# Nine attention stages on one core: the order of a step's work on TensorE, ScalarE and VectorE

## What is computed

```python
def _L2_xattn_ref(x1, x2, wq, wk, wv, wo, bo):
    q = (x1 @ wq.T).reshape(b, n, HEADS, HEAD_DIM).transpose(0, 2, 1, 3)
    k = (x2 @ wk.T).reshape(b, m, HEADS, HEAD_DIM).transpose(0, 2, 1, 3)
    v = (x2 @ wv.T).reshape(b, m, HEADS, HEAD_DIM).transpose(0, 2, 1, 3)
    dots = jnp.einsum('bhnd,bhmd->bhnm', q, k) * SCALE
    attn = jax.nn.softmax(dots, axis=-1)
    out = jnp.einsum('bhnm,bhmd->bhnd', attn, v)
    out = out.transpose(0, 2, 1, 3).reshape(b, n, DIM)
    return out @ wo.T + bo
...
x = x + _L2_xattn_ref(_layernorm(x, axis=-1), ctx_1024, ...)
```

## Time and profile before

| | us |
|---|---|
| median of 3 runs | 4896.71 |
| lowest, highest | 4893.21, 4901.27 |
| the profiled execution, its time | 4900.09 |
| the profiled execution, its span | 4898.2 |
| busy PE, DVE, POOL, ACT | 4007.7, 3203.4, 2994.6, 2059.5 |

### The profile page before, as it was taken

One profiled execution on the slowest core, in us unless ns is written; L12 is line 12 of the kernel. 1 busy time (PEld: TensorE's weight loads), 2 busy tenths in 40 slices (PEclk: granted clock), 3 DMA queues, 4 the chain that ended last, 5 costly groups with the idle time before them and its releaser, 6 DMA issues. The chain is left out here.

```text
span 4898.2 us, 215645 instructions
## 1 busy us (share of the span) xinstructions
PE 4007.7 (82%) x85067; PEld 2918.6 (60%) x85076; DVE 3203.4 (65%) x10848; ACT 2059.5 (42%) x5737; POOL 2994.6 (61%) x4949
## 2 busy tenths in 40 slices
PE   8999977254899978656999997559879998889988
PEld 6777754132566666523777774335547776667766
DVE  5875668422344688787556874753337878888866
ACT  4555545011344444365555554112225543336632
POOL 6766632276455699688556762038876777777710
PEclk9999988555899998755999997879998999999999
DMA  3000012433100022200000002113431000000000
GB/s 94 5 13 19 19 28 57 78 62 54 37 0 0 18 39 39 35 1 1 2 0 15 22 18 54 42 46 75 77 62 35 0 15 16 16 9 1 0 13 24
DMA packets 380509, 139.58 MB, mean 28 GB/s; under 512 B 216487, under 2 KB 373239, under 8 KB 380055
## 3 DMA queue, kind: packets, MB, share of 16 engines
q1 hardware_dynamic: 345430, 107.60, 9.3%
q0 software_dynamic: 34816, 28.34, 4.0%
HBM read 91.46 MB, written 43.85 MB: 28 GB/s over the span
## 5 line engine op out<-in xcount | busy, mean ns | idle before, releaser
L1051 DVE TENSOR_REDUCE rowmax<-ps 128x16 f32<-128x1024 f32 x512 | 626.3, 1223 | 488.0 <-PE ps L678 487.7
L696 PE MATMUL ps<-prob,kT 32*64 32x256 f32 x9216 | 781.7, 408 | 8.7 <-issue 2.4
L721 PE MATMUL ps<-v,probT 64*64 64x64 f32 x36864 | 764.6, 227 | 5.3 <-issue 2.2
L721 PEld LDWEIGHTS ps<-v,probT 64*64 64x64 f32 x36864 | 683.8, 140 | 57.4 <-issue 16.0
L678 PE MATMUL ps<-kblock,qT 32*64 32x256 f32 x8192 | 697.0, 410 | 17.2 <-DVE rowmax L1060 14.2
L900 ACT ACTIVATE probT<-ps 128x1024 f32<-128x1024 f32 x512 | 518.0, 1012 | 353.4 <-PE ps L708 353.0
L585 POOL TENSOR_TENSOR kblock<-kT,key_scale 128x512 f32<-128x512 f32 x576 | 599.8, 1041 | 18.2 <-ACT kT L878 7.6
L587 POOL TENSOR_TENSOR prob<-qT,key_scale 128x512 f32<-128x512 f32 x576 | 601.5, 1044 | 0.0
L561 POOL TENSOR_TENSOR vareps<-moments,eps 128x1 f32<-128x1 f32 x522 | 98.8, 189 | 745.7 <-DVE negmean L1025 745.6
L887 ACT ACTIVATE xn<-x_res,nmr,rstd 128x128 f32 (+1 forms) x512 | 252.7, 494 | 513.6 <-POOL nmr L567 349.5
L708 PEld LDWEIGHTS ps<-mT,pick_bf 32*64 32x64 bf16 x16384 | 311.7, 108 | 221.2 <-ACT mT L857 74.1
(11 more groups left out here) (380 smaller groups left out, 9655.7 us busy)
## 6 DMA issues: line engine op xcount, KB each, us to landing
ctxT<-in_ctxT SPq DMA_DIRECT2D x256, 64.0 KB, 1.8
held<-in_g_w SPq DMA_DIRECT2D x16, 836.0 KB
ctxT<-in_ctxT SPq DMA_DIRECT2D x256, 32.0 KB, 1.9
table<-prob SPq DMA_DIRECT2D x32, 256.0 KB, 2.4
x_dram<-x_res SPq DMA_DIRECT2D x32, 256.0 KB, 2.4
x_res<-x_dram SPq DMA_DIRECT2D x16, 512.0 KB, 6.9
x_res<-in_x SPq DMA_DIRECT2D x8, 512.0 KB, 7.5
x_res<-in_e_w SPq DMA_DIRECT2D x64, 64.0 KB
```

The source lines that it names most:

```text
L696: mm = nc.tensor.matmul(out.rearrange("p (h s) -> p h s", h=GH), k.kT[rows, buf, S * b:S * b + S], k.qblock[rows, buf, :, S * b:S * b + S] ...
L721: mm = nc.tensor.matmul(k.ps_o[S * b:S * b + S, u, S * hh:S * hh + S], k.probT[rows, buf, at:at + S], k.v9[rows, buf, (HD + 1) * h:(HD + 1 ...
L1051: nc.vector.tensor_reduce(spread, heads, AX.X, ALU.max).then_inc(soft.did["max_raw"], 1)
```

## The change

On TensorE a step now begins with queries and keys, the transposed `xn` and the transposed maxima; then come eight waits in a row; then y, the values and the transposed result; then mask rows and scores; the mixing is last. The first scores' bank is awaited by `max_raw` and no longer by `max_done`. The maxima are subtracted ahead of the second scores' products and no longer behind them. All softmax stages but L1_xattn make the values by one product, and the copies that take them out exchange the rows of heads 8 to 15: three instructions (128 x 64, and twice 64 x 64 elements) for one, on ScalarE or on VectorE. ScalarE does the front copies ahead of the value-side copies and no longer writes the doubled columns of `xnT`. VectorE does L1051's maxima ahead of the division, and the two differences last. In L3_xattn, the masked scores' addition stands in the place of the maxima.

```diff
--- before.py
+++ after.py
@@ -643,6 +643,15 @@
+WHOLE = (slice(0, P), slice(0, HEADS), slice(0, P))
...
+def value_parts():
+
+    first, second, low, high = slice(0, HEADS // 2), slice(HEADS // 2, HEADS), slice(0, S), slice(S, P)
+    return [(slice(0, P), first, slice(0, P)), (low, second, high), (high, second, low)]
...
-                    start=not part.softmax or first, stop=not part.softmax, tile_position=place)
+                    start=not part.softmax, stop=not part.softmax or groups == low, tile_position=place)
...
-                    start=False, stop=groups == low and h == GH - 1, tile_position=place)
+                    start=groups == high and h == 0 and not part.added, stop=False, tile_position=place)
...
-    def values_mixable(mixes, it, mb):
-        if mixes is not None:
-            after(pe, c, "exp_done", it, mb)
-            after(pe, c, "v_done", it, mb)
-            after(pe, c, "on_done", it, mb + 1)
-
-    def scores_writable(score1, score2, it):
-        if score1 is not None:
-            after(pe, c, "max_done", it, 4)
-            after(pe, c, "kblock_done", it, 3)
-        if score2 is not None:
-            after(pe, c, scores_read(c, it, 6), it, 6)
-            after(pe, c, "qblock_done", it, 5)
-
...
         less = score2 if score2 is not None and score2.softmax else None
 
         mm = None
-        if value is not None or turn is not None or out is not None:
-            after(pe, c, values_read(c, it, 4), it, 4)
-            after(pe, c, "y_read", it, 9)
-            after(pe, c, "oT_done", it, 8)
-        if out is not None:
-            mm = nc.tensor.matmul(k.ps_y, k.oT[:, b8, :], weights(out, 3), start=True, stop=True)
-        if value is not None:
-            source, wv = k.ctxT[:, b3, :] if value.cross else k.xnT[:, b3, :], weights(value, 2)
-            if value.softmax:
-                nc.tensor.matmul(k.ps_v[:, 0:S], source[:, 0:P], wv[:, 0:S], start=True, stop=True)
-                mm = nc.tensor.matmul(k.ps_v[:, S:P], source[:, S:S + P], wv[:, S:P], start=True, stop=True)
-            else:
-                mm = nc.tensor.matmul(k.ps_v, source[:, 0:P], wv, start=True, stop=True)
-        if turn is not None:
-            after(pe, c, "on_done", it, 7)
-            mm = nc.tensor.transpose(k.ps_oT, k.o[:, b7, :], k.ident)
-        if mm is not None:
-            mm.then_inc(c.yv_psum, 1)
-
-        mm = None
+        if mixes is not None:
+            after(pe, c, "v_done", it, mb)
         after(pe, c, "kT_done", it, 3)
         if c.steady is None:
...
-        early = less is None or any(part is not None and part.added for part in (score1, score2))
-        if less is None:
-            values_mixable(mixes, it, mb)
-            scores_writable(score1, score2, it)
         if norm is not None:
             after(pe, c, "xn_done", it, 1)
             mm = nc.tensor.transpose(k.ps_xT, k.xn[:, b1, :], k.ident)
         if less is not None:
-            values_mixable(mixes, it, mb)
-            if early:
-                scores_writable(score1, score2, it)
             after(pe, c, "max_done", it, 5)
             mm = nc.tensor.matmul(k.ps_mT, top_halves(k.rowmax[:, b5, :]), k.ident_bf[:, :], start=True, stop=True)
         if mm is not None:
             mm.then_inc(c.front_psum, 1)
 
+        mm = None
+        if score1 is not None:
+            after(pe, c, "max_raw", it, 4)
+            after(pe, c, "kblock_done", it, 3)
+        if score2 is not None:
+            after(pe, c, scores_read(c, it, 6), it, 6)
+            after(pe, c, "qblock_done", it, 5)
         if mixes is not None:
-            for hh in range(HEADS // 2):
-                mm = mix(mixes, (par - mb) % NB, hh)
-            mm.then_inc(mixes.did["o_psum"], 1)
-        if not early:
-            scores_writable(score1, score2, it)
+            after(pe, c, "exp_done", it, mb)
+        if value is not None or turn is not None or out is not None:
+            after(pe, c, values_read(c, it, 4), it, 4)
+            after(pe, c, "y_read", it, 9)
+            after(pe, c, "oT_done", it, 8)
+        if out is not None:
+            mm = nc.tensor.matmul(k.ps_y, k.oT[:, b8, :], weights(out, 3), start=True, stop=True)
+        if mixes is not None and turn is None:
+            after(pe, c, "on_done", it, mb + 1)
+        if value is not None:
+            source, wv = k.ctxT[:, b3, :] if value.cross else k.xnT[:, b3, :], weights(value, 2)
+            if value.name == "L1_xattn":
+                nc.tensor.matmul(k.ps_v[:, 0:S], source[:, 0:P], wv[:, 0:S], start=True, stop=True)
+                mm = nc.tensor.matmul(k.ps_v[:, S:P], source[:, S:S + P], wv[:, S:P], start=True, stop=True)
+            else:
+                mm = nc.tensor.matmul(k.ps_v, source[:, 0:P], wv, start=True, stop=True)
+        if turn is not None:
+            after(pe, c, "on_done", it, 7)
+            mm = nc.tensor.transpose(k.ps_oT, k.o[:, b7, :], k.ident)
+        if mm is not None:
+            mm.then_inc(c.yv_psum, 1)
+
         for bk in range(2):
             if score1 is not None and score1.added:
                 add_rows(score1, k.s1, 0, bk)
@@ -810,11 +804,11 @@
         if score1 is not None:
             query_scores(score1, b3, low).then_inc(score1.did["low_rows"], 1)
         if score2 is not None:
-            mm = key_scores(score2, b5, high, first=not score2.added)
             if less is not None:
                 after(pe, c, "mT_done", it, 5)
                 for h in range(GH):
-                    mm = less_max(less, b5, h, high)
+                    less_max(less, b5, h, high)
+            mm = key_scores(score2, b5, high)
             mm.then_inc(score2.did["first_rows"], 1)
 
         if score1 is not None:
@@ -822,11 +816,16 @@
             query_scores(score1, b3, high).then_inc(score1.did["s1_psum"], 1)
         if score2 is not None:
             after(pe, c, "first_rows", it, 5)
-            mm = key_scores(score2, b5, low, first=False)
             if less is not None:
                 for h in range(GH):
-                    mm = less_max(less, b5, h, low)
+                    less_max(less, b5, h, low)
+            mm = key_scores(score2, b5, low)
             mm.then_inc(score2.did["s2_psum"], 1)
+
+        if mixes is not None:
+            for hh in range(HEADS // 2):
+                mm = mix(mixes, (par - mb) % NB, hh)
+            mm.then_inc(mixes.did["o_psum"], 1)
...
-        if turn is not None:
-            act.wait_ge(c.yv_psum, it - 2)
-            after(act, c, "y_read", it, 8)
-            if c.name(it, 3) in VALUE_BIAS:
-                after(act, c, values_read(c, it, 3), it, 3)
-            nc.scalar.activation(k.oT[:, b7, :], k.ps_oT, ACT.Copy).then_inc(turn.did["oT_done"], 1)
-        if value is not None and value.name not in VALUE_BIAS:
-            act.wait_ge(c.yv_psum, it - 2)
-            after(act, c, "y_read", it, 8)
-            after(act, c, "o_psum", it, 3 + NB)
-            nc.scalar.activation(values(k, b3), heads_of(k.ps_v), ACT.Copy).then_inc(value.did["v_done"], 1)
...
-                if not norm.cross:
-                    nc.scalar.activation(k.xnT[:, b1, P:P + S], k.ps_xT[:, 0:S], ACT.Copy)
...
+        if turn is not None:
+            act.wait_ge(c.yv_psum, it - 2)
+            after(act, c, "y_read", it, 8)
+            if c.name(it, 3) in VALUE_BIAS:
+                after(act, c, values_read(c, it, 3), it, 3)
+            nc.scalar.activation(k.oT[:, b7, :], k.ps_oT, ACT.Copy).then_inc(turn.did["oT_done"], 1)
+        if value is not None and value.name not in VALUE_BIAS:
+            act.wait_ge(c.yv_psum, it - 2)
+            after(act, c, "y_read", it, 8)
+            after(act, c, "o_psum", it, 3 + NB)
+            for rows, heads, source in value_parts():
+                mm = nc.scalar.activation(values(k, b3)[rows, heads, :], heads_of(k.ps_v)[source, heads, :], ACT.Copy)
+            mm.then_inc(value.did["v_done"], 1)
...
-                nc.vector.tensor_tensor(values(k, b3), heads_of(k.ps_v), heads_of(bias),
-                                        ALU.add).then_inc(value.did["v_done"], 1)
+                for rows, heads, source in value_parts() if value.softmax else [WHOLE]:
+                    mm = nc.vector.tensor_tensor(values(k, b3)[rows, heads, :], heads_of(k.ps_v)[source, heads, :],
+                                                 heads_of(bias)[source, heads, :], ALU.add)
+                mm.then_inc(value.did["v_done"], 1)
...
+        if soft is not None:
+            after(dve, c, "s1_psum", it, 3)
+            spread = k.rowmax[:, b3, :].rearrange("p (f c r) -> p c f r", f=2, c=2)[:, :, :, 0:GH]
+            heads = k.s1.rearrange("p c (f h s) -> p c f h s", f=2, h=GH)
+            nc.vector.tensor_reduce(spread, heads, AX.X, ALU.max).then_inc(soft.did["max_raw"], 1)
+        if plain is not None:
...
         mixes, mb = c.mixing(it)
         if mixes is not None and mixes.softmax:
...
         if soft is not None:
```

(7 more changed lines are left out.)

22 lines of the change are left out of this document (10 added, 12 removed).

## The result

| | before | changed |
|---|---|---|
| median, us | 4895.19 (4 runs) | 5049.84 (4 runs) |
| lowest, highest | 4893.21, 4901.27 | 5045.93, 5054.98 |
| span of the profiled execution | 4898.2 | 5050.4 |

The changed kernel takes 1.0314 times as long (95% interval 1.0297 to 1.0332), 155 us more. The forecast was 5025 us.

What follows compares the result with a forecast made beforehand. It took the exponential's wait ahead of y to close a one-step loop of 4.97 us in L0_attn; stage changes summed to +2.03 us, times 64 +130, giving 5025 us, with a range of 4870 to 5100.

Steps and rivals of the forecast that it cites:

- The loop of one step: Exponential, y, values, transposed result, addition of y, statistics, GpSimd, `xn`, next exponential: closed by the change, 4.97 us in L0_attn.
- The wait's price: On TensorE ahead of y: 0.12 us for each of three waits behind the exponential's.
- the first link: From the exponential's end on ScalarE to y on TensorE: 0.05 us plus three waits, 0.41 us.
- The loop's edge: The end of the four-step code loop, taken to add 0.05 us to the mean step.
- the value pieces on VectorE: L0_xattn, L1_attn, L3_attn: three instructions ahead of the statistics take 0.45 us (0.33 to 0.6), where one took 0.20.
- TensorE's saving: TensorE's step in L1_attn: 0.17 us from one values product plus 0.23 of idle time, 6.50 to 6.10 us.
- the idle time: TensorE's idle time ahead of the maxima's product in L0_xattn, L1_attn and L2_attn: 0.23 us to go.
- The forecast's own range: Whole kernel: bounds on L992's release, the pieces, the loop's end and the wait make 4930 to 5110 us.
- The differences meet GpSimd: VectorE's differences, placed last beside GpSimd's long products, lengthen six stages by 0.3 us: 5140 us, chance 0.07.
- TensorE alone: Rival: no loop closes or its waits come early enough; stages run at TensorE's own work: 4737 us, chance 0.12.
- Maxima subtracted first: TensorE's subtraction ahead of the second scores: same products, maxima's copy covered by y, values and transposed result: nothing.
- the copies' order on ScalarE: ScalarE's three value copies lie between front copies and `xn`, where it waits for GpSimd anyway: nothing.

Runs made afterwards that it cites:

- e1: Changed kernel with TensorE's wait for the exponential moved behind y and the values, ahead of the transposed result: 4814.69 us.
- e2: Changed kernel with the exponential's wait put last in the row ahead of y, on y's product itself in three of four steps: 4945.78 us.
- e3: Changed kernel with VectorE adding the values' bias in one instruction, not three; leaves out a row exchange, so for timing only: 4984.49 us.
- e9: e5 with y, values and transposed result first in TensorE's step, the exponential's wait at the second scores (maxima's product with added rows): 4919.99 us.
- e10: e9 with L0_xattn's values made by one product and their bias added in three pieces, as in the changed kernel: 4924.43 us.
- e7: Kernel before with the part on the maxima alone: max_raw awaited, maxima ahead of the division, differences last; TensorE's order as before: 5149.41 us.
- e6: Changed kernel with its value part undone: two half products, one copy or addition, doubled columns of xnT: 5072.25 us.
- e11: e5 with the two differences of the maxima made a step later, behind the statistics: 4769.53 us.
- e4: Kernel before with the value part alone: one product, three copies or additions, no doubled columns of xnT; order and waits as before: 4942.43 us.
- e12: Changed kernel with its part on the maxima undone: first scores' bank awaited by max_done, maxima behind the division, differences behind them: 5684.17 us.
- e8: e5 with the two differences of the maxima made a step later, right behind the addition of y, except in L1_xattn: 4837.99 us.
- e5: Changed kernel, exponential's wait ahead of the transposed result with added rows, else behind it; L0_xattn and L3_attn values by halves, bias whole: 4787.37 us.

## Why the prediction was right, and where it was not

**Direction and mechanism: right, shown.** The loop of one step is in the trace of the changed kernel link by link, and e1 opens it and wins back more than the loss. The wait's price as part of the first link is shown by e2. At that each wait instruction was counted as 0.12 us three times, and the trace has 0.11 four times.

**The links.** Exponential to y 0.41, measured 0.43 to 0.50; y to the end of the transposed result 0.82, measured 0.79; to the addition of y 0.12, measured 0.14 to 0.21; to L567 2.05, measured 2.07; to the exponential 0.52, measured 0.52. L0_attn, L2_attn and L2_xattn came out 0.06 to 0.08 above 4.97, L3_ffn 0.05 above 5.56. The loop's edge was taken as 0.05 and adds nothing.

**Mis-sized: the value pieces on VectorE.** I took 0.45 us for three, between 0.33 and 0.6. They take 0.72, 0.52 more than the one (e3), outside my own bounds: a small instruction costs even more than the whole one, by 0.04. The step that failed is the upper bound "each as much as the whole": the earlier trace rows had the price of one addition of 128 x 128 elements and no row of a smaller one, on 128 partitions or on 64. It accounts for 0.27 of the 0.33 and 0.35 us by which L0_xattn and L3_attn were missed; the rest is the 0.06 to 0.08 of the loop itself.

**L1_xattn: 0.12 us, where nothing was forecast.** The window before was 6.04, after 6.16, and 6.01 and 5.98 in e1 and e2. That speaks for the exponential's wait in this stage too, but e9 and e10, which have the same code there, differ by 0.08. There is another candidate: TensorE's granted clock, which goes to and fro between 2.4 and 1.2 GHz in this window, was 0.83 of the higher on average, for 0.90 before. The clock alone does not order the runs: it is 0.86 in e1 and e2 and 0.91 in e7, and all three take about 6.00 us. No run tells the two apart, and it stays open. The prediction took the stage as untouched and had named more than 0.1 us here as a sign of being wrong; that step of it failed.

**The masked stages.** TensorE's saving was forecast as 0.17 + 0.23 in L1_attn and measured at 0.35 in all. e6 shows the product's 0.17 there (6.32 for 6.15), so the idle time gave 0.18 and not 0.23.

**The total came out nearer than its terms.** By the table the steady steps grew by 3.14 us, 201 us over 64 steps, against 2.03 and 130 forecast. From the first `xn` of each stage to its last it is 165 us, and the whole 155: outside the steady middle a step lost less, presumably because the pipeline isn't full when a chain fills, empties or changes its stage. I had multiplied by 64 throughout. One error was 71 us too low, the other some 46 too high, so that 25 us of error are left is in part luck.

**The forecast's own range.** Its four bounds, taken together at their ends, make about 4890 to 5145 us and not 4930 to 5110. The measured time lies in both.

**The differences meet GpSimd.** They did, as the rival said: L1067 took 0.95 us. They ended 0.47 us ahead of the addition of y, against the 0.45 of slack that I had counted, so it cost nothing. In e1, where that slack is gone, the addition of y does stand right behind them, and e11 gains by moving them.

**TensorE alone (4737 us).** e1 comes nearer to it by one moved wait, 4814.69 us, and e11 is at 4769.53; none reached it.

**Costed at nothing and true only together.** "Maxima subtracted first ... nothing" and the copies' order on ScalarE hold in the order of the full change. In e9 the subtraction waits for the copy of the maxima, in e4 that copy waits for the pieces. e4, e7, e9 and e12 each take a cover away and cost 49 to 634 us.

## What to carry to other kernels

When a wait is moved ahead of other work of an engine that runs its instructions in order, follow that work to its readers and back to the signal: if the signal's producer stands behind them on any engine, the wait has closed a loop of one step, and its length, not the engines' busy time, is the step. Put a late wait on the first instruction that needs it and last among its neighbours, and look at what each edit covers, since the parts of an order change don't add up: here the value part was -22 or +49 us, and the maxima's part +257 alone and -634 in company. Splitting a small VectorE copy for the sake of TensorE costs a whole instruction for each piece.

## What the runs showed of the hardware

- Each wait instruction of TensorE's queue, that of the late signal and those behind it, took 0.11 us (0.47 us from the exponential to y with four of them, 0.05 with none), and the records stand 0.11 us apart.
- A VectorE addition from PSUM of 128 x 64 or 64 x 64 elements held VectorE at least as long as one of 128 x 128: 0.24 us on average for each of three, and 0.20 us (changed kernel and e3).
- The difference of 128 x 16 elements took 0.16 to 0.17 us alone (e8, e11), and up to 1.04 beside GpSimd's 1.04 us product (e1).
- In e2 the step behind the turn of the four-step loop had 0.53 us from the exponential to y, for 0.05 in the other three: there the late signal is awaited first, by a register operation, and two wait instructions and two more register operations stand behind it.
- In e9 L0_attn's scores and subtractions on TensorE took from 154.23 to 156.40, 2.17 us, where e5 has them in 1.75. A wait for the maxima's copy stands between the first scores and the subtractions in e9; whether it is the cause wasn't tried apart.
